# Adaptive-norm attention and mixture of experts on one core: the three-part split of q and k dealt to three engines

## The chip, the cores and the metric

The kernel runs on one core of one Trainium2 chip. The metric is device time in microseconds (us). Every time below is from one profiled execution, except where it says that it is a median of runs.

## The reference

The input x is 8 sequences of 256 tokens with 128 channels. A conditioning vector per sequence gives shifts, scales and gates (sa, ca, ga, sb, cb, gb).

```
h = layernorm(x) * (1 + ca) + sa
x = x + ga * attention(h)        # 16 heads of 8 channels, band of +-128 keys
h = layernorm(x) * (1 + cb) + sb
x = x + gb * moe(h)              # 8 experts, top 2, silu(h w1) * (h w3), then w2
```

In attention the keys before the first and after the last token are zeros that still count in the softmax's denominator: a query gets one term exp(0 - max) for each such padding key inside its band.

## The kernel before, in words

All five engines run programs of their own, in order, and meet at semaphores. Attention is a software pipeline over the 8 sequences b. Every engine loops `for step in range(-AHEAD, B + 4)` with AHEAD = 2, and inside it `for j in range(NPAIR)` with NPAIR = 8 pairs of heads. In one step the engines work on several sequences at once: sequence step + 2 is projected to q, k and v and packed, sequence step has its row maxima taken (`scores_A`, then `row_max` on VectorE), sequence step - 1 has its scores made again with the maximum taken off, its exponentials and its weighted values (`scores_B` on TensorE, `exps` on ScalarE, `mask_probs` on GpSimd, `weigh_values` on TensorE), sequence step - 2 is transposed and normalised (`o_T`, `normalise_attn`, `attn_T`), sequence step - 3 goes through the output projection, the gate and the second layernorm, and step - 4 through the router (`logits`, `top2`). "Step 4" in this text is step == 4 of this loop; it begins where VectorE takes the first row maximum of sequence 4.

q and k must be exact to nearly fp32 but are multiplied in bf16, so each is split in three bf16 parts: part 0 is the bf16 cast, part 1 the cast of the residual, part 2 the cast of what then remains. The parts lie in `parts[P, 2, 3, L]`. SyncE's queue stores them to HBM in 12 transfers (6 of part 0, 4 of part 1, 2 of part 2, line 291) and reads them back stacked along the contraction (`fill_stacks`, lines 303 and 306). Before the change ScalarE makes part 0 (`cast_part`, line 407), and VectorE does the rest: `split(b, 0)` after the row maximum of j=5 (lines 758 and 762), `split(b, 1)` after that of j=6 (line 765).

The row maxima go back into the stack of q as well: `half_max` on VectorE, `max_T` on TensorE, `m_copy` on ScalarE, and `store_max(b, half)` on SyncE's queue (line 279). TensorE's `scores_B` of j=0 waits for half 0 (semaphore `m_in0`), that of j=4 for half 1 (`m_in1`).

SyncE's queue is written out by hand, in this order in each step: `load_experts` (steps 2 to 5, 1.5 MB each, lines 311 and 312), `store_max(step-1, 1)`, `fill_stacks(step+1)`, `store_part(step+2, 0)`, `store_part(step+2, 1)`, `store_max(step, 0)`, `store_part(step+2, 2)`, `broadcast_mod_rows(step)`, the store of h2 for sequence step - 3. A wait in it holds all that stands behind it.

One bank of PSUM, `psM`, is handed from user to user (`take_psM`): the next matmul into it waits until the last reader is done. So `logits` at j=6 waits for `normalise_attn`, and `attn_T` at j=7 for the copy of the logits at the head of `top2`. After attention a routing stage and a loop over 39 tiles of tokens and experts follow, which the change doesn't touch.

## Time and profile before

| | |
|---|---|
| median of 3 runs | 379.56 us (377.26 to 380.9) |
| the profiled execution | 377.73 us |
| its span in the trace | 376.0 us |
| attention, to the end of the last step | to about 200 us |
| routing and expert loop | about 200 us to 376 us |
| busy: TensorE, VectorE, ScalarE, GpSimd | 286.6, 248.8, 172.6, 167.6 us |

The span is what the trace shows; the execution's time is 1.73 us longer. A busy time is a share of one engine's program; engines overlap. In the rows, PE is TensorE, PEld its weight loads, DVE VectorE, ACT ScalarE, POOL GpSimd and SPq the queue of SyncE. A row of a timeline gives start and duration, then in brackets how long the engine had been idle and which instruction released it.

### The profile page before, as it was taken

Reading aid. Unit: us, or ns where it says so; the run is one execution under the profiler, and the core shown is the slowest. Engines: PE = TensorE matmul, PEld = TensorE weight load, DVE = VectorE, ACT = ScalarE, POOL = GpSimd, SP = SyncE. Lnnn points to the kernel's source line nnn. Section 1 sums busy time; section 2 is a strip of 40 time slices with the busy share of each in tenths; the row PEclk is TensorE's granted clock in tenths of the full one; section 3 lists DMA queues with packets and bytes.
Section 4 is the critical chain, followed back from the end, with each engine's and each line's share of the span. In section 5 each row is a group of like instructions: output and inputs, shape, how many; then the busy total and the mean of one; then the engine's idle time right before and its main releaser. Section 6 shows DMA issues by size and latency. Waiting matters only on the chain. (4 is left out here: it accounts for less than half of the span.)

```text
span 376.0 us, 7095 instructions
## 1 busy us (share of the span) xinstructions
PE 286.6 (76%) x2281; PEld 207.8 (55%) x2281; DVE 248.8 (66%) x699; ACT 172.6 (46%) x360; POOL 167.6 (45%) x247
## 2 busy tenths in 40 slices
PE   4647798999889989999862349899888888888400
PEld 2223354455545545555441239888888888888400
DVE  5749787889986797987467964355555555444165
ACT  7312366666564746676710123444444444444150
POOL 3400143346452445556630242666566656664321
PEclk9999699999996989999975557999999999999955
DMA  4566355876676634101000001111111111111182
GB/s 113 149 159 149 79 133 163 219 216 152 189 190 181 169 97 110 58 1 51 17 15 14 1 22 23 42 44 42 35 42 42 42 37 40 42 42 28 38 241 84
DMA packets 38008, 32.98 MB, mean 88 GB/s; under 512 B 4456, under 2 KB 31992, under 8 KB 37984
## 3 DMA queue, kind: packets, MB, share of 16 engines
q1 hardware_dynamic: 35168, 27.17, 27.3%
q0 software_dynamic: 2496, 5.12, 5.2%
q10 hardware_dynamic: 320, 0.40, 0.4%
q8 instruction: 12, 0.20, 0.2%
q14 instruction: 12, 0.10, 0.1%
HBM read 21.64 MB, written 10.96 MB: 87 GB/s over the span
## 5 line engine op out<-in xcount | busy, mean ns | idle before, releaser
L788 DVE TENSOR_REDUCE negm<-psA 128x4 f32<-128x1024 f32 x64 | 78.1, 1222 | 20.7 <-PE psA L1157 19.7
L428 ACT ACTIVATE probs<-psB 128x512 f32<-128x512 f32 x128 | 72.3, 596 | 41.8 <-PE psB L1179 41.4
L576 POOL TENSOR_SCALAR_AFFINE_SELECT probs<-probs 128x512 f32<-128x512 f32 x64 | 42.3, 686 | 62.9 <-ACT probs L428 62.8
L1314 PE MATMUL psA<-kd,probs 128*128 128x128 f32 x416 | 54.5, 287 | 13.0 <-DVE kd L1019 12.6
L666 POOL DMA_INDIRECT y_d<-kd,sca_idx x39 | 40.7, 1044 | 43.9 <-ACT kd L492 37.7
L1314 PEld LDWEIGHTS psA<-kd,probs 128*128 128x128 f32 x416 | 51.3, 201 | 15.3 <-DVE kd L1019 14.7
L1154 PE MATMUL psA<-kd,qs 96*128 96x512 bf16 x128 | 49.6, 409 | 7.2 <-DMA kd<-stack_d 5.2
L1179 PE MATMUL psB<-qs,kd 98*128 98x256 bf16 x256 | 47.1, 283 | 1.9 <-DMA qs<-mT 1.1
L1019 DVE COPY kd<-psO 128x128 f32<-128x128 f32 x39 | 11.4, 292 | 55.2 <-remote 27.0
L661 POOL DMA_INDIRECT kd<-h_d,gat_idx x39 | 38.1, 976 | 18.5 <-issue 9.1
L1323 PE MATMUL psM<-probs,kd 128*128 128x128 f32 x312 | 41.3, 275 | 0.4 <-ACT kd L492 0.4
L1199 PE MATMUL psO<-probs,vx 128*32 128x256 f32 x512 | 38.0, 395 | 0.3 <-POOL probs L576 0.3
L1323 PEld LDWEIGHTS psM<-probs,kd 128*128 128x128 f32 x312 | 37.9, 192 | 0.6 <-DVE kd L1025 0.6
L496 ACT COPY probs<-w_sb 128x512 f32 x39 | 24.1, 619 | 29.1 <-issue 29.0
L1157 PE MATMUL psA<-mask_b,ident_b 128*128 128x256 bf16 x128 | 37.0, 289 | 0.0
L1179 PEld LDWEIGHTS psB<-qs,kd 98*128 98x128 bf16 x256 | 24.2, 103 | 16.5 <-ACT probs L428 3.4
L1154 PEld LDWEIGHTS psA<-kd,qs 96*128 96x128 bf16 x128 | 13.1, 102 | 30.6 <-issue 10.5
L492 ACT COPY kd<-psM 128x128 f32<-128x128 f32 x39 | 10.4, 266 | 40.9 <-PE psM L1323 34.2
L1314 PE MATMUL psB<-kd,probs 128*128 128x128 f32 x208 | 25.4, 275 | 0.0
L1314 PEld LDWEIGHTS psB<-kd,probs 128*128 128x128 f32 x208 | 24.3, 192 | 0.0
L1031 DVE COPY probs<-w_sb 128x512 f32 x39 | 16.8, 430 | 5.3 <-issue 5.2
L1199 PEld LDWEIGHTS psO<-probs,vx 128*32 128x32 f32 x512 | 12.0, 109 | 13.5 <-issue 9.9
(186 smaller groups left out, 410.1 us busy)
## 6 DMA issues: line engine op xcount, KB each, us to landing
stack_d<-parts SPq DMA_DIRECT2D x96, 64.0 KB, 2.1
w_sb<-in_L_ffn_experts_w_dram SPq DMA_DIRECT2D x12, 512.0 KB, 6.5
qs<-stack_d SPq DMA_DIRECT2D x8, 384.0 KB, 4.1
kd<-stack_d SPq DMA_DIRECT2D x16, 192.0 KB, 4.8
mod_sb<-mod_d SPq DMA_DIRECT2D x8, 320.0 KB, 4.2
probs<-y_d SPq DMA_DIRECT2D x8, 256.0 KB, 5.0
h_d<-h SPq DMA_DIRECT2D x8, 128.0 KB, 1.8
out_dram<-probs SPq DMA_DIRECT2D x4, 256.0 KB, 2.3
```

The source lines that it names most:

```text
L428: nc.scalar.activation(probs[:, kt, n % PRING], psB[:, kt, :].rearrange("p (h q) -> p h q", h=H2), ACT.Exp).then_inc(s["exped"], 1)
L496: nc.scalar.copy(w3_t[:, r], w3_sb[:, bass.ds(e, 1), :].rearrange("c o i -> c (o i)")).then_inc(s["w3_ready"], 1)
L576: nc.gpsimd.affine_select(out=u, in_=u, compare_op=ALU.is_ge, fill=0.0, base=0, pattern=[[0, 2 * H2], [-sign, P]], channel_multiplier=sign ...
L661: pool.indirect_dma_start(xs[:, r], None, h2_d, bass.IndirectOffsetOnAxis(ap=gat_idx[:, n:n + 1], axis=0)).then_inc(gathered[r], 16)
L666: pool.indirect_dma_start(y_d, bass.IndirectOffsetOnAxis(ap=sca_idx[:, n:n + 1], axis=0), ys[:, r], None).then_inc(scattered[r], 16)
L788: nc.vector.tensor_reduce(negm[:, b % 2, :, :, j], psA[:, n % 2].rearrange("p q (h k) -> p q h k", h=H2), AX.X, ALU.max, negate=True).then ...
L1154: nc.tensor.matmul(psA[:, n % 2, qt, :].rearrange("p (h k) -> p h k", h=H2), qs[0:SROWS, r, j, qt * P:(qt + 1) * P], kd[0:SROWS, r, :, j, ...
L1157: last = nc.tensor.matmul(psA[:, n % 2, qt, :].rearrange("p (h k) -> p h k", h=H2)[:, :, off:off + P], ident_b[:], mask_b[:, qt], start=Fa ...
L1179: last = nc.tensor.matmul(psB[:, kt, h * L:(h + 1) * L], kd[0:SROWS + H2, r, h, j, kt * P:(kt + 1) * P], qs[0:SROWS + H2, r, j, :], start= ...
L1199: last = nc.tensor.matmul(psO[32 * g:32 * g + 32, half, :], vx[:, b % VRING, kt, j, h, :], probs[:, kt, j, h, :], start=(piece == 0), stop ...
L1314: last = nc.tensor.matmul(ps[:, k * P:(k + 1) * P], w[:, r, k * P:(k + 1) * P], xsT[:, r], start=True, stop=True)
L1323: last = nc.tensor.matmul(psY, hid[:, r, k * P:(k + 1) * P], w2_t[:, r, k * C:(k + 1) * C], start=(k == 0), stop=(k == NC - 1))
```

## The change

- `cast_part1`: part 1's cast goes from VectorE to ScalarE, ahead of the exponentials of j=6.
- `part2`: the last subtraction goes to GpSimd, behind the masks of j=7, for sequences 2 to 7; for the first two it stays on VectorE (`part2_first`). `residual` is what is left on VectorE.
- `pad_term` goes from VectorE to GpSimd, at j=4 behind `h2_scale`.
- VectorE's paired small operations become one each, or two for four in `values`; for this the bias of v is loaded twice side by side, one transfer more at the start.

```diff
...
@@ -267,7 +267,8 @@
...
             sp.dma_start(wv_sb[:], wv).then_inc(s["wv_in"], 16)
-            sp.dma_start(bv_sb[:], bv.partition_broadcast(P)).then_inc(s["wv_in"], 16)
+            for kt in range(2):
+                sp.dma_start(bv_sb[:, kt], bv.partition_broadcast(P)).then_inc(s["wv_in"], 16)
...
@@ -281,10 +282,7 @@
...
-                if part == 0:
-                    sp.wait_ge(s["part_cast"], b + 1)
-                else:
-                    sp.wait_ge(s["residuals"], 3 * b + 1 + part)
+                sp.wait_ge(s[("part_cast", "part1_cast", "part2_ready")[part]], b + 1)
...
@@ -393,7 +391,7 @@
...
                 if b >= 1:
-                    act.wait_ge(s["residuals"], 3 * b)
+                    act.wait_ge(s["resid_ready"], b)
...
@@ -405,6 +403,10 @@
...
                 nc.scalar.copy(parts[:, :, 0, :], qkf[:]).then_inc(s["part_cast"], 1)
+            def cast_part1(b):
+                act.wait_ge(s["resid_ready"], b + 1)
+                nc.scalar.copy(parts[:, :, 1, :], resid[:]).then_inc(s["part1_cast"], 1)
...
@@ -413,7 +415,7 @@
...
                 if b >= 3:
-                    act.wait_ge(s["den_steps"], 3 * (b - 2))
+                    act.wait_ge(s["pad_ready"], b - 2)
...
@@ -464,6 +466,8 @@
...
                         cast_part(step + AHEAD)
+                    if j == (4 if step == -AHEAD else 6) and has(step + AHEAD):
+                        cast_part1(step + AHEAD)
...
@@ -575,6 +579,23 @@
...
                                             pattern=[[0, 2 * H2], [-sign, P]], channel_multiplier=sign).then_inc(s["masked"], 1)
+            def part2(b):
+                pool.wait_ge(s["part1_cast"], b + 1)
+                nc.gpsimd.tensor_tensor(parts[:, :, 2, :], resid[:], parts[:, :, 1, :], ALU.subtract).then_inc(s["part2_ready"], 1)
+            def pad_term(b):
+                pool.wait_ge(s["emin_ready"], 2 * b + 2)
+                if b == 0:
+                    pool.wait_ge(s["consts"], 5)
+                if b >= 1:
+                    pool.wait_ge(s["den_steps"], 2 * b - 1)
+                for qt in range(2):
+                    last = nc.gpsimd.tensor_scalar(
+                        den[:, 0, qt, :].rearrange("p (f q h) -> p f h q", f=2, h=H2),
+                        emin[:, b % 3, :, qt], npad[:, qt:qt + 1], 0.0, ALU.mult, ALU.add)
+                last.then_inc(s["pad_ready"], 1)
...
@@ -640,6 +661,10 @@
...
                         h2_shift(step - 3)
+                    if j == 4 and has(step - 2):
+                        pad_term(step - 2)
+                    if j == 7 and step > 1 - AHEAD and has(step + AHEAD):
+                        part2(step + AHEAD)
...
@@ -751,33 +776,30 @@
...
-            def split(b, i):
-                if i == 0:
-                    dve.wait_ge(s["part_cast"], b + 1)
-                    nc.vector.tensor_tensor(resid[:], qkf[:], parts[:, :, 0, :], ALU.subtract).then_inc(s["residuals"], 1)
-                    dve.wait_ge(s["residuals"], 3 * b + 1)
-                    if b >= 1:
-                        dve.wait_ge(s["parts_stored"], NSTORES * 16 * b)
-                    nc.vector.tensor_copy(parts[:, :, 1, :], resid[:]).then_inc(s["residuals"], 1)
-                else:
-                    dve.wait_ge(s["residuals"], 3 * b + 2)
-                    nc.vector.tensor_tensor(parts[:, :, 2, :], resid[:], parts[:, :, 1, :], ALU.subtract).then_inc(s["residuals"], 1)
+            def residual(b):
+                dve.wait_ge(s["part_cast"], b + 1)
+                if b >= 1:
+                    dve.wait_ge(s["part2_ready"], b)
+                nc.vector.tensor_tensor(resid[:], qkf[:], parts[:, :, 0, :], ALU.subtract).then_inc(s["resid_ready"], 1)
+            def part2_first(b):
+                dve.wait_ge(s["part1_cast"], b + 1)
+                nc.vector.tensor_tensor(parts[:, :, 2, :], resid[:], parts[:, :, 1, :], ALU.subtract).then_inc(s["part2_ready"], 1)
...
             def values(b):
...
-                    dve.wait_ge(s["wv_in"], 32)
+                    dve.wait_ge(s["wv_in"], 48)
...
-                for kt in range(2):
-                    for par in range(H2):
-                        last = nc.vector.tensor_tensor(
-                            vx[:, b % VRING, kt, :, par, D * par:D * par + D],
-                            psM[:, kt * C:(kt + 1) * C].rearrange("p (q h d) -> p q h d", h=H2, d=D)[:, :, par, :],
-                            bv_sb[:].rearrange("p (q h d) -> p q h d", h=H2, d=D)[:, :, par, :], ALU.add)
+                for par in range(H2):
+                    last = nc.vector.tensor_tensor(
+                        vx[:, b % VRING].rearrange("p k q h c -> p (k q) h c")[:, :, par, D * par:D * par + D],
+                        psM[:, 0:2 * C].rearrange("p (q h d) -> p q h d", h=H2, d=D)[:, :, par, :],
+                        bv_sb[:].rearrange("p k (q h d) -> p (k q) h d", h=H2, d=D)[:, :, par, :], ALU.add)
...
             def row_max(b, j):
@@ -795,53 +817,33 @@
...
-                for qt in range(2):
-                    last = nc.vector.tensor_scalar(negmb[:, b % 2, half, qt], negm[:, b % 2, qt, :, 4 * half:4 * half + 4],
-                                                   0.0, None, ALU.min)
-                last.then_inc(s["half_max"], 1)
-            def pad_term(b):
-                dve.wait_ge(s["emin_ready"], 2 * b + 2)
-                if b == 0:
-                    dve.wait_ge(s["consts"], 5)
-                for qt in range(2):
-                    last = nc.vector.tensor_scalar(
-                        den[:, 0, qt, :].rearrange("p (f q h) -> p f h q", f=2, h=H2),
-                        emin[:, b % 3, :, qt], npad[:, qt:qt + 1], None, ALU.mult)
-                last.then_inc(s["den_steps"], 1)
+                nc.vector.tensor_scalar(negmb[:, b % 2, half], negm[:, b % 2, :, :, 4 * half:4 * half + 4],
+                                        0.0, None, ALU.min).then_inc(s["half_max"], 1)
...
             def normalise_attn(b):
-                dve.wait_ge(s["den_steps"], 3 * b + 1)
+                dve.wait_ge(s["pad_ready"], b + 1)
...
-                for qt in range(2):
-                    ps = late(b)[:, qt * 256:(qt + 1) * 256].rearrange("p (q r) -> p q r", r=VCOL)
-                    last = nc.vector.tensor_tensor(
-                        den[:, 1, qt, :].rearrange("p (q h) -> p q h", h=H2), ps[:, :, 16:18],
-                        den[:, 0, qt, :].rearrange("p (q h) -> p q h", h=H2), ALU.add)
-                last.then_inc(s["den_steps"], 1)
-                dve.wait_ge(s["den_steps"], 3 * b + 2)
+                ps = late(b)[:, 0:2 * L].rearrange("p (q r) -> p q r", r=VCOL)
+                nc.vector.tensor_tensor(den[:, 1].rearrange("p t (q h) -> p (t q) h", h=H2), ps[:, :, 16:18],
+                                        den[:, 0].rearrange("p t (q h) -> p (t q) h", h=H2), ALU.add).then_inc(s["den_steps"], 1)
+                dve.wait_ge(s["den_steps"], 2 * b + 1)
...
-                dve.wait_ge(s["den_steps"], 3 * b + 3)
+                dve.wait_ge(s["den_steps"], 2 * b + 2)
...
-                for qt in range(2):
-                    ps = late(b)[:, qt * 256:(qt + 1) * 256].rearrange("p (q r) -> p q r", r=VCOL)[:, :, 0:16]
-                    last = nc.vector.tensor_tensor(
-                        attn[:, qt, :].rearrange("p (q h d) -> p q h d", h=H2, d=D),
-                        ps.rearrange("p q (h d) -> p q h d", d=D),
-                        den[:, 2, qt, :].rearrange("p (q h o) -> p q h o", h=H2, o=1).broadcast_to([P, NPAIR, H2, D]),
-                        ALU.mult)
-                last.then_inc(s["normed"], 1)
+                nc.vector.tensor_tensor(
+                    attn[:].rearrange("p t (q h d) -> p (t q) h d", h=H2, d=D),
+                    ps[:, :, 0:16].rearrange("p q (h d) -> p q h d", d=D),
+                    den[:, 2].rearrange("p t (q h o) -> p (t q) h o", h=H2, o=1).broadcast_to([P, 2 * NPAIR, H2, D]),
+                    ALU.mult).then_inc(s["normed"], 1)
...
             def gate_attn(b):
...
-                for t in range(2):
-                    nc.vector.tensor_tensor(t1[:, t], late(b)[:, t * C:(t + 1) * C], mod_sb[:, b, 0, :],
-                                            ALU.mult).then_inc(s["t1_ready"], 1)
+                nc.vector.tensor_tensor(t1[:], late(b)[:, 0:2 * C].rearrange("p (t c) -> p t c", c=C),
+                                        mod_sb[:, b, 0:1, :].broadcast_to([P, 2, C]), ALU.mult).then_inc(s["t1_ready"], 2)
...
             def x1_last(b):
...
@@ -923,8 +925,8 @@
...
                     if j == 4 and step == -AHEAD:
-                        split(0, 0)
-                        split(0, 1)
+                        residual(0)
+                        part2_first(0)
...
@@ -941,12 +943,10 @@
...
                         h2_last(step - 3)
-                    if j == 4 and has(step - 2):
-                        pad_term(step - 2)
                     if j == 5 and step > -AHEAD and has(step + AHEAD):
-                        split(step + AHEAD, 0)
-                    if j == 6 and step > -AHEAD and has(step + AHEAD):
-                        split(step + AHEAD, 1)
+                        residual(step + AHEAD)
+                    if j == 7 and step == 1 - AHEAD:
+                        part2_first(1)
...
```

## Rows read from the trace of the kernel before

**Rows 1.** Windows, one step each (steps 2 to 6): span, busy times, clock, DMA, GB/s.
```profile
58.62:77.36 18.74, 17.25 (x148) 9.07 (x148) 15.14 (x35) 12.48 (x26) 6.10 (x11) 1.00 0.71 190
77.36:96.88 19.52, 17.71 (x154) 10.00 (x154) 17.48 (x43) 12.46 (x27) 10.89 (x18) 1.00 0.65 178
96.88:120.11 23.23, 20.97 (x160) 11.74 (x161) 18.77 (x56) 12.68 (x27) 10.32 (x18) 0.87 0.73 187
120.11:142.15 22.04, 20.13 (x160) 11.26 (x159) 17.56 (x49) 12.67 (x27) 9.57 (x16) 0.90 0.56 157
142.15:158.57 16.42, 16.28 (x150) 9.09 (x149) 14.82 (x42) 10.69 (x23) 8.35 (x17) 1.00 0.32 81
```

**Rows 2.** Timeline of TensorE, step 4, j=6 and j=7: start, us, engine line [idle before].
```profile
112.60 0.61 PE L1236 MATMUL psM<-gate_sb,h2T 128*128 128x8 f32 x4 [1.37 <-DVE attn L830]
...
114.42 0.69 PE L1215 MATMUL psM<-ident,attn 128*128 128x128 f32 x2 [0.40 <-DVE lg L886]
114.90 0.63 PE L1154 MATMUL psA<-kd,qs 96*128 96x512 bf16 x1
```

**Rows 3.** Timeline of VectorE, step 4, j=5 to j=7.
```profile
110.03 0.67 DVE L758 TENSOR_TENSOR resid<-qkf,parts 128x512 f32<-128x512 f32 x1
110.73 0.74 DVE L762 CAST parts<-resid 128x512 bf16<-128x512 f32 x1
...
113.60 0.68 DVE L765 TENSOR_TENSOR parts<-resid,parts 128x512 bf16<-128x512 f32 x1
```

**Rows 4.** Timeline of TensorE, steps 1 to 4: first scores of a step or half.
```profile
41.64 1.04 PE L1179 MATMUL psB<-qs,kd 98*128 98x256 bf16 x4 [0.28 <-DMA qs<-mT]
...
58.75 0.44 PE L1126 MATMUL psM<-ident,xn 128*128 128x128 f32 x2 [1.00 <-DVE xn L706]
...
68.72 0.39 PE L1179 MATMUL psB<-qs,kd 98*128 98x256 bf16 x2 [0.78 <-DMA qs<-mT]
...
106.47 0.38 PE L1179 MATMUL psB<-qs,kd 98*128 98x256 bf16 x2
```

**Rows 5.** Timeline of SyncE's queue, from steps 1 to 4.
```profile
58.16 1.51 SPq L291 DMA_DIRECT2D stack_d<-parts  x2
...
60.34 0.94 SPq L311 DMA_DIRECT2D w_sb<-in_L_ffn_experts_w_dram  x2
...
95.60 1.17 SPq L291 DMA_DIRECT2D stack_d<-parts  x2
...
97.92 1.03 SPq L311 DMA_DIRECT2D w_sb<-in_L_ffn_experts_w_dram  x2
```

**Rows 6.** Page, DMA issues: count, KB each, us to landing.
```profile
w_sb<-in_L_ffn_experts_w_dram SPq DMA_DIRECT2D x12, 512.0 KB, 6.5
```

**Rows 7.** Timeline of GpSimd, steps 1 and 3, the masks after j=7.
```profile
57.40 1.22 POOL L576 TENSOR_SCALAR_AFFINE_SELECT probs<-probs 128x512 f32<-128x512 f32 x2 [1.49 <-ACT probs L428]
...
95.66 1.22 POOL L576 TENSOR_SCALAR_AFFINE_SELECT probs<-probs 128x512 f32<-128x512 f32 x2 [1.49 <-ACT probs L428]
```

**Rows 8.** Groups by form, GpSimd's additions.
```profile
L589 POOL TENSOR_TENSOR x_sb<-t,x_sb 128x256 f32<-128x256 f32 x7 | 5.1, 732 | 11.6 <-DVE t L843 11.6
...
L583 POOL TENSOR_TENSOR x_sb<-x_sb,mod_sb 128x128 f32<-128x128 f32 x16 | 7.0, 454 | 0.0
```

**Rows 9.** Groups by form, VectorE and ScalarE.
```profile
L777 DVE TENSOR_TENSOR vx<-psM,bv_sb 128x64 f32<-128x64 f32 x32 | 4.9, 217 | 2.7 <-PE psM L1142 2.5
...
L407 ACT CAST parts<-qkf 128x512 bf16<-128x512 f32 x8 | 4.9, 619 | 1.4 <-DMA stack_d<-parts 1.3
...
L762 DVE CAST parts<-resid 128x512 bf16<-128x512 f32 x8 | 4.7, 584 | 0.3
```

**Rows 10.** Timeline of all engines, step 9.
```profile
191.40 0.65 DVE L809 TENSOR_SCALAR den<-emin,npad 128x16 f32<-128x16 f32 x2
191.57 0.87 POOL L601 TENSOR_TENSOR h2m<-xn,mod_sb 128x128 f32<-128x128 f32 x2 [0.72 <-DVE xn L881]
...
193.31 0.69 PE L1215 MATMUL psA<-ident,attn 128*128 128x128 f32 x2 [2.13 <-DVE attn L830]
```

More of the change, by code:

```diff
@@ L127, in adaln_attention_moe @@
         bqk = sb("bqk", [P, 4])
-        bv_sb = sb("bv_sb", [P, C])
+        bv_sb = sb("bv_sb", [P, 2, C])
         stats = sb("stats", [P, NT, 6])
@@ L240, in adaln_attention_moe @@
             "ln1_steps veps_ok rstd_ok stack_const0 stack_const1 vx_zero vx_ones "
-            "xn_ready xnT_ps hT_ready qk_ps qkf_ready part_cast residuals parts_stored v_ps v_ready "
+            "xn_ready xnT_ps hT_ready qk_ps qkf_ready part_cast part1_cast resid_ready part2_ready parts_stored v_ps v_ready "
             "scoresA rowmax half_max mT_ps mT_ready emin_ready m_in0 m_in1 "
-            "scoresB exped masked pv o_ready oT_ps den_steps normed aT_ps aT_ready op_ps t1_ready xg_ready x1_ready "
+            "scoresB exped masked pv o_ready oT_ps pad_ready den_steps normed aT_ps aT_ready op_ps t1_ready xg_ready x1_ready "
             "ln2_steps rs2_ready xn2_ready h2m_ready h2_ready h2T_ps h2T_ready lg_ps lg_ready top_ready h2_stored0 h2_stored1"
@@ L1138, in project_v @@
                 if b == 0:
-                    pe.wait_ge(s["wv_in"], 32)
+                    pe.wait_ge(s["wv_in"], 48)
                 take_psM("v_ready", b + 1)
```

## The prediction

> **What bounds the kernel now.** I read the windows first, one for each step of attention, since only attention is changed. In step 6, with nothing left to project or pack, TensorE is busy for 16.28 of 16.42 us: it sets that step, and step 7 is like it. Steps 2 to 5 last 18.74 to 23.23 us, and TensorE's idle time in them is 1.49, 1.81, 2.26 and 1.91 us. In steps 4 and 5 the granted clock is 0.87 and 0.90 as well: part of the time was at the lower of its two levels, 1.2 GHz [rows 1]. Reckoned at full speed that loses 0.13 x 23.23 = 3.0 and 0.10 x 22.04 = 2.2 us. So there are 7.5 us of idle time and 5.2 us of clock in these four steps, and nothing else that a better division of work could win; VectorE's 75 to 90% matters only where TensorE waits for it.
>
> Then I read TensorE's timeline at the end of step 4 for who releases it. It is idle for 1.37 us until attn is normalised, then for 0.40 us until the logits are copied, and from 114.90 the same matmuls take 0.63 us each [rows 2]: the clock fell behind these two waits. VectorE shows why: residual and cast, 0.67 + 0.74 us, stand ahead of the normalisation, and the third part, 0.68 us, ahead of the copy [rows 3]. Elsewhere a wait of 1.00 us stands alone, and the matmul behind it is at full speed with 0.44 us [rows 4].
>
> Last I read the waits that do not end on a compute engine. Scores of j=4 in step 2 waited 0.78 us for a transfer, the second half of the row maxima; in step 4 they start at 106.47 without a wait. The first scores of step 1 also waited for such a store, the other half, 0.28 us [rows 4].
>
> **The change, part by part.** *VectorE.* Per step it loses the cast (0.58 us mean; 0.74 us in step 4), the third part (0.68 us) [rows 3, 9] and the padding term (0.65 us in step 9) [rows 10]. Of the merges, four adds of values (217 ns each alone, overlapping in a row) become two: 0.1 us; row maxima, denominators, attn and gate give some 0.3 us together, my estimate from the same overlap. In all 2.1 to 2.4 us a step. On TensorE's path lie only the cast (0.74) and about 0.1 us ahead of the normalisation, and the subtraction ahead of the copy: the wait of 1.37 becomes 0.4 to 0.6 and that of 0.40 becomes 0.2 us. If the two waits no longer throw the clock, 3.0 + 2.2 us come back too.
>
> *ScalarE.* One cast more, 0.62 us as its twin [rows 9]. It stands in front of the exponentials of j=6 and waits for the residual, and behind it TensorE waits for the exponentials' PSUM. ScalarE has some 12.7 busy us in 23 [rows 1]; while the residual is made it has nothing to do. Cost 0 to 0.2 us a step, taken as 0.1 within the waits below. Part 1's four stores go out behind part 0's six in either case.
>
> *The extra load of the bias and the first steps.* One issue of some 0.5 us on SyncE's queue at the start, where the queue later waits for the first cast anyway: nothing. Step 0 gets about 1.3 us off VectorE, but the first scores of step 1 wait for the stored row maxima already [rows 4], and that store stands behind the same stores of parts: gain nothing; step 1 likewise, up to 0.3 us.
>
> *GpSimd, the third part.* The trace has no such subtraction of 512 columns on GpSimd. Bounds: 0.68 us, VectorE's own [rows 3], and 1.46 us, twice the 732 ns of 256 columns. The two additions (454 ns for 128 columns, 732 for 256) give 176 ns + 2.17 ns a column, so 1.29 us [rows 8]; I take 1.3. The Trainium skill, GPSIMD Engine Reference, section "3.1 Elementwise — side-by-side cycle accounting", gives such an operation 1.96 times VectorE's time, which would be an estimate of 1.33 us here; the sum would not move.
>
> Its length is not the point, its place is. It comes behind the masks of j=7, which wait for the last exponentials: they start at 95.66 and end at 96.88 [rows 7]. So the third part is ready at about 98.2. Its stores went out at 95.60, and they head a row on SyncE's queue: stores of part 2, broadcast of the modulation, the store of h2, the expert weights at 97.92 [rows 5], and behind these the second half of the row maxima. All that moves by 98.2 - 95.6 = 2.6 us. In step 2 it moves by 57.40 + 1.22 + 1.3 + 0.05 - 58.16 = 1.8 us [rows 5, 7].
>
> The row maxima are a small store behind 1.5 MB of weights. In step 2 TensorE could go on 68.72 - 60.34 = 8.4 us after the first of the weights was issued [rows 4, 5]; the weights take 6.5 us to land [rows 6], and the third of them is issued some 1.0 us after the first, so the delay is at least 7.5 us. The Trainium skill says in DMA: Bandwidth & Descriptors, section "Queues, rings and completion order", that each DMA engine consumes descriptors in ring order; by that rule a small store cannot pass the weights, and the row of 68.72 agrees. Without it the store would land early and the stall below would be zero.
>
> With 8.4 us, step 4's weights go out at 100.5, the maxima are there at 108.9, and TensorE wants them at 106.47 less some 0.4 us from shorter waits before: a stall of 2.8 us. With 7.5 us and the shorter subtraction it is 1.3 us. Step 2: 0.78 + 1.8 = 2.6 us. Step 3 has one issue less ahead of the weights: 2.4. Step 5: as step 4, 2.8. While TensorE stands, VectorE catches up, so the later waits shrink further. Step by step, idle plus clock loss now against then, with 0.4, 0.5, 1.2 and 0.7 us for waits that remain: step 2, 1.5 to 3.0; step 3, 1.8 to 2.9; step 4, 5.3 to 4.0; step 5, 4.1 to 3.5. Sum +1.5 +1.1 -1.3 -0.6 = +0.7 us.
>
> *GpSimd, the padding term.* In steps 1 to 7 it fits between `h2_scale` and the next masks. In step 9 it does not: `h2_scale` runs until 191.57 + 0.87 = 192.44, two small operations follow (no row for them; at most the 0.65 us of VectorE, at least 0.2; I take 0.4), and only then may VectorE normalise, which it now does behind its own padding term, from 192.05. TensorE is already waiting for it there, 2.13 us [rows 10]. Cost 0.8 us, less 0.2 of merges: +0.6 (0.2 to 0.9). Sum so far +1.3 us.
>
> *The clock.* A stall of 2.4 to 2.8 us in one piece is longer than the 1.37 + 0.40 us that preceded a fall [rows 2], and longer than the 1.00 us that did not [rows 4]. So I expect it to fall behind these stalls in about two of the four steps. One fall cost 3.0 or 2.2 us; less some 0.6 us of waits that it covers, 2.0 each: +4 us. Together +5.3: 377.73 + 5.3 = 383.0 against the profiled execution, and with the 1.83 us by which the median lies above it, 384.9; I say 384.5.
>
> **The rivals.** *B, the stall comes and the clock holds.* +1.3 us: 380.9. For it: I know no place where one wait of this length stands alone in full work.
>
> *C, faster.* The same relief with a short stall. It decides at about 1.2 us: between the 1.00 us behind which the clock held and the 1.77 us behind which it fell. With 1.0 us in each step (the maxima landing 7.5 us after the weights, or the third part ready near 0.7 us) idle and clock are 1.4, 1.5, 2.2 and 1.7 us, against 1.5, 1.8, 5.3 and 4.1: -5.9, +0.6 at the end, so -5.3: 374.3. For it: steps 3 and 4 of before show no wait for the maxima, so the delay might be under 8.4 us there. Against it: the bounds must all fall on one side.
>
> *D, the clock falls in all four steps, or the last step costs more.* +9: 388.5.
>
> **How the numbers follow.** Forecast A (two or so falls) 0.40, D 0.07, B 0.25, C 0.28. A measurement of this kernel tells about 1% from no change, 3.8 us. A lies over that by its middle (part of it under), D over, B within, C partly within. Faster 0.25, same 0.31, slower 0.44. The range takes in C and nearly D, 373.5 to 389.5; the forecast's own is 382 to 388.
>
> **What would show it.** In the profile after: TensorE's wait for the store of the row maxima at j=4 in steps 2 to 5 grows from 0.8 us in all to about 10; the cast on ScalarE 0.62 us, the subtraction on GpSimd 1.3 us; the waits for attn and logits in steps 4 and 5 nearly gone; the low-clock stretch behind j=4 instead of j=6; in step 9 VectorE waits some 0.8 us for GpSimd. I am wrong if the maxima land less than 7.5 us after the weights are issued, or if GpSimd's masks of j=7 end before the store of part 2 was due.

## The result and the profile after

The changed kernel takes 386.57 us, the median of 4 runs (384.71 to 390.52), where the kernel before took 378.55 us in 4 runs on the same chip (377.26 to 380.9). The ratio is 1.0205, with a 95% interval of 1.0164 to 1.0247: 2% slower. One of the 4 runs, the one of 390.52 us, was in a slower state of the chip and is left out of the ratio. The profiled run of the changed kernel is one of 385.87 us with a span of 384.1 us, against 376.0 us before; the two profiles differ by 8.1 us.

These are the windows of the changed kernel for steps 2 to 5, in the columns of [rows 1]: span, busy time of TensorE, its weight loads, VectorE, ScalarE and GpSimd, granted clock, DMA share, GB/s.

```profile
59.92:81.63 21.71, 18.67 (x148) 9.94 (x148) 14.06 (x24) 13.23 (x27) 8.04 (x16) 0.92 0.62 165
81.63:102.52 20.89, 17.82 (x154) 9.92 (x154) 15.71 (x32) 13.21 (x28) 11.13 (x22) 1.00 0.62 168
102.52:126.26 23.74, 19.91 (x158) 10.86 (x158) 17.19 (x46) 13.20 (x28) 11.71 (x23) 0.93 0.57 153
126.26:147.44 21.18, 18.32 (x160) 10.59 (x161) 15.39 (x39) 13.31 (x28) 9.89 (x20) 1.00 0.66 172
```

Against [rows 1], VectorE has 1.1 to 2.2 us less to do in each step, and still three of the four steps are longer (step 5 is 0.9 us shorter). TensorE's idle time, span less busy, is 3.04, 3.07, 3.83 and 2.86 us where it was 1.49, 1.81, 2.26 and 1.91. The clock now falls in steps 2 and 4 instead of 4 and 5. The list of waits names what TensorE waits for; its columns are the us of all such waits, their number and the longest, from 40 to 200 us:

```profile
PE psB L1179 <- DMA qs<-mT: 11.9, 6, 2.8
...
DVE den L827 <- POOL den L595: 5.1, 4, 2.9
```

The first row is the row maxima, coming back from memory. Two of the six waits are for their first half, at j=0 of steps 1 and 2 (1.79 us, which was 0.28, and 0.84 us, which was none). The other four are for the second half: the first scores of j=4 in steps 2 to 5. In TensorE's timeline they answer to the third of [rows 4], which had 0.78 us, and to the fourth, which had no wait:

```profile
71.72 0.39 PE L1179 MATMUL psB<-qs,kd 98*128 98x256 bf16 x2 [1.72 <-DMA qs<-mT]
...
93.89 0.39 PE L1179 MATMUL psB<-qs,kd 98*128 98x256 bf16 x2 [2.44 <-DMA qs<-mT]
...
115.08 0.39 PE L1179 MATMUL psB<-qs,kd 98*128 98x256 bf16 x2 [2.80 <-DMA qs<-mT]
...
138.35 0.39 PE L1179 MATMUL psB<-qs,kd 98*128 98x256 bf16 x2 [2.34 <-DMA qs<-mT]
```

Their sum is 9.30 us. Why the store comes late is to be read on SyncE's queue in step 4, which answers to [rows 5], and on GpSimd, which answers to [rows 7]:

```profile
104.26 1.18 SPq L289 DMA_DIRECT2D stack_d<-parts  x2
105.48 0.59 SPq L320 DMA_DIRECT2D mod_sb<-mod_d  x1
106.11 0.43 SPq L343 DMA_DIRECT2D h_d<-h  x1
106.59 1.03 SPq L309 DMA_DIRECT2D w_sb<-in_L_ffn_experts_w_dram  x2
107.66 0.47 SPq L310 DMA_DIRECT2D w_sb<-in_L_ffn_experts_w_dram  x1
108.17 0.68 SPq L280 DMA_DIRECT2D qs<-mT  x1
```

```profile
101.89 1.22 POOL L580 TENSOR_SCALAR_AFFINE_SELECT probs<-probs 128x512 f32<-128x512 f32 x2 [1.62 <-ACT probs L430]
103.08 1.15 POOL L585 TENSOR_TENSOR parts<-resid,parts 128x512 bf16<-128x512 f32 x1
```

The masks of j=7 end at 103.1, the third part follows until 104.23, and the stores of part 2 leave 0.03 us later. Everything below stands behind them in the program of SyncE: modulation, h2, the three issues of expert weights, and at 108.17 the row maxima. TensorE goes on at 115.08, 8.49 us after the first of the weights. In steps 2, 3 and 5 this delay is 8.20, 8.04 and 8.61 us.

The trace also has the moment at which each store's semaphore is raised. In steps 2 to 5 the store of the row maxima lands 5.05, 6.49, 6.86 and 7.01 us after its own issue, and TensorE starts 0.04 to 0.05 us behind it. The kernel before was already at the edge: in steps 3 and 4 the maxima landed 8.29 and 8.39 us after the first of the weights, in step 4 at 106.31, and TensorE wanted them at 106.47.

The groups by form price the moved operations, in the columns of [rows 9]:

```profile
L585 POOL TENSOR_TENSOR parts<-resid,parts 128x512 bf16<-128x512 f32 x6 | 6.9, 1154 | 5.9 <-ACT parts L409 5.9
...
L409 ACT CAST parts<-resid 128x512 bf16<-128x512 f32 x8 | 4.9, 616 | 8.0 <-DVE resid L783 7.9
...
L595 POOL TENSOR_SCALAR den<-emin,npad 128x16 f32<-128x16 f32 x16 | 4.2, 280 | 0.0
```

The subtraction of 512 columns takes 1.15 us on GpSimd, the cast on ScalarE 0.62 us, and a padding operation of 16 columns 0.28 us on GpSimd.

Two smaller losses lie outside these steps. The first is at the start, where the bias is loaded twice. SyncE's timeline and VectorE's:

```profile
9.27 2.55 SPq L275 DMA_DIRECT2D gate_sb<-in_L_ffn_gate_dram  x1
11.86 7.65 SPq L289 DMA_DIRECT2D stack_d<-parts  x12
```

```profile
12.86 0.49 DVE L715 BATCH_NORM_STATS2 stats<-x_sb 128x6 f32<-128x128 f32 x2 [3.61 <-DMA x_sb<-in_L_attn_x_dram]
```

The issue of the small gate load takes 2.55 us (0.92 before), the stores of the first part leave at 11.86 (10.95 before), and x of the next batch comes so late that VectorE waits 3.61 us for it. The first row maximum is taken at 27.94 instead of 26.86 us. The second is in the tail, step 9, and answers to [rows 10]:

```profile
197.06 0.86 POOL L622 TENSOR_TENSOR h2m<-xn,mod_sb 128x128 f32<-128x128 f32 x2 [0.72 <-DVE xn L883]
197.90 0.53 POOL L595 TENSOR_SCALAR den<-emin,npad 128x16 f32<-128x16 f32 x2
...
198.46 0.19 DVE L827 TENSOR_TENSOR den<-psA,den 128x32 f32<-128x32 f32 x1 [1.48 <-POOL den L595]
...
199.55 0.69 PE L1215 MATMUL psA<-ident,attn 128*128 128x128 f32 x2 [2.86 <-DVE attn L834]
```

GpSimd does the padding term only after `h2m`, VectorE waits 1.48 us for it, and TensorE waits 2.86 us for attn where it waited 2.13. From the last row maximum to the first matmul of the routing it is 33.05 us against 31.94.

By stretches, the 8.1 us are: start 1.1, steps 0 and 1 0.2, steps 2 to 5 4.0, steps 6 and 7 -0.2, tail 1.1, and 1.9 in routing and expert loop, whose code is the same in both kernels.

### The profile page after: what moved, and what is told of

Same layout as the page of the kernel before. It is cut to its first block and busy times, and to the rows that moved or that the text cites. A ratio compares the mean times of both kernels' runs of the same rounds, so it can differ in the third digit from the quotient of the medians.

```text
span 384.1 us, 7052 instructions
## 1 busy us (share of the span) xinstructions
PE 286.1 (74%) x2281; PEld 207.9 (54%) x2281; DVE 234.8 (61%) x613; ACT 177.8 (46%) x368; POOL 176.2 (46%) x269
## 3 DMA queue, kind: packets, MB, share of 16 engines
HBM read 21.71 MB, written 10.96 MB: 85 GB/s over the span
## 5 line engine op out<-in xcount | busy, mean ns | idle before, releaser
L580 POOL TENSOR_SCALAR_AFFINE_SELECT probs<-probs 128x512 f32<-128x512 f32 x64 | 39.4, 639 | 59.6 <-ACT probs L430 59.4
L1025 DVE TENSOR_TENSOR kd<-psA,kd 128x512 f32<-128x512 f32 x26 | 17.8, 686 | 2.3 <-PE psA L1314 1.6
```

Of the source, the lines that this page charges most:

```text
L580: nc.gpsimd.affine_select(out=u, in_=u, compare_op=ALU.is_ge, fill=0.0, base=0, pattern=[[0, 2 * H2], [-sign, P]], channel_multiplier=sign ...
```

## The experiments

Each kernel was timed against runs of the kernel before on the same chip. The chips differ (medians of the kernel before: 378.06 us for the first four experiments, 375.17 for the next four, 375.21 for the last two), so ratios are to be compared and not times. "First row maximum" below is the start of step 0's first one, and the sum of steps 2 to 5 runs from the first row maximum of step 2 to that of step 6: 83.53 us before and 87.52 changed. It comes from one profiled execution of each kernel.

**The third part back on VectorE.** Of the change all else stays.

```diff
+                    if j == 6 and step > -AHEAD and has(step + AHEAD):
+                        part2_first(step + AHEAD)      # VectorE
...
-                    if j == 7 and step > 1 - AHEAD and has(step + AHEAD):
-                        part2(step + AHEAD)            # GpSimd
```

> The changed kernel with the third part back on VectorE, ahead of j=7's work; all else as changed. Theory Q (the third part's stores, late on SyncE's queue, push the expert weights and behind them the row maxima): TensorE's wait for the row maxima at j=4 of steps 2 to 5 falls from 9.3 us to 1 to 2 us, and the time to 1.000 to 1.008 of the kernel before; what is left over 1.000 is the start (+1.1 us) and the last steps (+1.1 us). Rival G (the added cast on ScalarE and the padding term on GpSimd cost it, wherever the third part is): it stays at 1.015 to 1.022.

Measured: 375.46 us, ratio 0.9948 (0.9911 to 0.9984). One wait for the row maxima at j=4 is left, in step 2, as long as before:

```profile
70.76 0.39 PE L1173 MATMUL psB<-qs,kd 98*128 98x256 bf16 x2 [0.81 <-DMA qs<-mT]
```

Steps 2 to 5 take 77.07 us. So the one moved subtraction turns the rest of the change from 0.5% faster into 2% slower. The wait is a little under the expected 1 to 2 us. The ratio is 0.5% under the expected range, which allowed 1.1 us for the start; in this kernel the start cost 0.2 us (first row maximum at 27.02).

**The expert weights behind the row maxima.** The changed kernel, with the two weight loads of a step issued after the loads of the stacks instead of ahead of the row maxima. GpSimd keeps the third part.

```diff
-                if 2 <= step < 2 + E // 2:
-                    load_experts(2 * (step - 2))
...
                     fill_stacks(step + AHEAD - 1)
+                if 2 <= step < 2 + E // 2:
+                    load_experts(2 * (step - 2))
```

> The changed kernel, third part on GpSimd as changed, but the expert weights issued behind the row maxima and the filling of the stacks of the same step. Theory Q: the third part is as late as before, yet the row maxima have no weights in front of them; the wait at j=4 falls to under 0.5 us in all, the clock holds behind j=4, and the time is 0.995 to 1.006 of the kernel before. Rival L (what costs is that the third part itself is late, because the stacks are filled late): no gain, 1.015 to 1.022. Rival G: the same, 1.015 to 1.022.

Measured: 372.17 us, ratio 0.9861 (0.9827 to 0.9896). SyncE's timeline in step 4, then the windows of steps 2 to 5:

```profile
97.74 1.18 SPq L289 DMA_DIRECT2D stack_d<-parts  x2
98.96 0.59 SPq L320 DMA_DIRECT2D mod_sb<-mod_d  x1
99.59 0.43 SPq L343 DMA_DIRECT2D h_d<-h  x1
100.29 0.68 SPq L280 DMA_DIRECT2D qs<-mT  x1
101.07 0.33 SPq L301 DMA_DIRECT2D qs<-stack_d  x1
101.44 0.89 SPq L304 DMA_DIRECT2D kd<-stack_d  x2
102.38 0.94 SPq L309 DMA_DIRECT2D w_sb<-in_L_ffn_experts_w_dram  x2
```

```profile
59.35:77.71 18.36, 17.09 (x148) 9.15 (x148) 14.06 (x24) 13.06 (x27) 8.06 (x16) 1.00 0.70 195
77.71:96.00 18.29, 17.64 (x154) 10.00 (x154) 15.63 (x33) 13.08 (x28) 11.56 (x22) 1.00 0.69 191
96.00:115.82 19.82, 18.27 (x158) 10.36 (x158) 17.25 (x46) 13.41 (x28) 12.13 (x22) 1.00 0.66 185
115.82:134.84 19.02, 18.34 (x160) 10.66 (x161) 15.29 (x39) 13.19 (x28) 10.27 (x19) 1.00 0.69 191
```

The stores of part 2 leave as late as in the changed kernel, behind the masks, 1.74 us after the start of step 4 in both; the row maxima now go out at 100.29, ahead of the weights at 102.38. No wait at j=4 is left in any step, and the clock is 1.00 in all four. They take 75.49 us, 12.0 less than in the changed kernel. The store of the maxima now lands 2.0 to 2.5 us after its issue, and not 5.0 to 7.0. So the late third part does its harm through the weights in front of the maxima. The gain is larger than was expected (0.995 to 1.006).

**The kernel before with the same move of the weights.** It separates what the order alone brings from what the relief of VectorE brings once the order is mended.

```diff
-                if 2 <= step < 2 + E // 2:
-                    load_experts(2 * (step - 2))       # ahead of the row maxima
...
+                if 2 <= step < 2 + E // 2:
+                    load_experts(2 * (step - 2))       # behind fill_stacks
```

> The kernel before with the expert weights issued behind the row maxima and the stacks. Theory Q: only the wait of 0.78 us in step 2 is there to be won; 0.996 to 1.001. If the weights in this place hold up the stores of the parts instead, 1.003 to 1.010.

Measured: 377.06 us, ratio 0.9967 (0.9946 to 0.9987). Windows of steps 4 and 5:

```profile
97.55:118.83 21.28, 18.37 (x158) 10.38 (x158) 19.02 (x57) 12.56 (x27) 10.29 (x17) 1.00 0.64 181
118.83:139.32 20.49, 18.23 (x159) 10.50 (x160) 17.52 (x49) 12.56 (x27) 8.85 (x15) 1.00 0.61 175
```

The waits for attn and for the logits are still there in both steps, 1.37 and 0.40 us, as in [rows 2]. But the clock did not fall behind them in this execution; over the ten runs the mean granted clock goes from 0.896 to 0.921, and this one is at the upper end. Steps 2 to 5 take 79.25 us here (to the first row maximum of step 6 at 139.49; the window shown ends 0.17 us earlier) and 75.49 us with the relief of VectorE: in these two profiles the relief is worth 3.8 us, and the two ratios differ by 1.1%. The changed kernel hides it behind its stalls. The ratio is in the expected range. Of the 4.3 us between 79.25 and the 83.53 of the kernel before, most is the clock that did not fall, and the medians show only 0.3%.

**The kernel before with only the third part on GpSimd.** Cast, padding term and all small operations stay as before.

```diff
-                    if j == 6 and step > -AHEAD and has(step + AHEAD):
-                        split(step + AHEAD, 1)         # VectorE
...
+                    if j == 7 and step > 1 - AHEAD and has(step + AHEAD):
+                        part2(step + AHEAD)            # GpSimd, behind the masks
```

> The kernel before with one part of the change alone: the third part of sequences 2 to 7 on GpSimd behind the masks of j=7. Theory Q: the waits for the row maxima at j=4 are 8 to 11 us in all, as in the changed kernel, and the time is 1.008 to 1.020 of the kernel before. Rival G: VectorE is relieved of 0.68 us a step, so 0.990 to 1.003.

Measured: 388.69 us, ratio 1.0278 (1.0248 to 1.0307). The same four first scores of j=4:

```profile
70.03 0.61 PE L1187 MATMUL psB<-qs,kd 98*128 98x256 bf16 x2 [2.15 <-DMA qs<-mT]
...
93.67 0.61 PE L1187 MATMUL psB<-qs,kd 98*128 98x256 bf16 x2 [2.65 <-DMA qs<-mT]
...
117.31 0.61 PE L1187 MATMUL psB<-qs,kd 98*128 98x256 bf16 x2 [2.60 <-DMA qs<-mT]
...
141.43 0.61 PE L1187 MATMUL psB<-qs,kd 98*128 98x256 bf16 x2 [3.11 <-DMA qs<-mT]
```

The loss comes with this one move and is larger without the relief: 10.51 us of waits, and behind each of the four the two scores take 0.61 us instead of 0.39, which is the lower clock. Steps 2 to 5 take 95.29 us. The waits are in the expected range of 8 to 11 us; the time lies over it (1.008 to 1.020), as the clock fell in all four steps.

**The third part ahead of the masks of j=7.** The changed kernel; the subtraction stays on GpSimd and is only issued before the masks.

```diff
+                    if j == 7 and step > 1 - AHEAD and has(step + AHEAD):
+                        part2(step + AHEAD)
                     if j % 2 == 1 and has(step - 1):
                         mask_probs(step - 1, j - 1)
...
-                    if j == 7 and step > 1 - AHEAD and has(step + AHEAD):
-                        part2(step + AHEAD)
```

> The changed kernel with GpSimd's third part issued ahead of the masks of j=7 instead of behind them, so that it no longer waits for the last exponentials; same instruction, same engine, weights where they were. Theory Q: its place and not its length costs; the waits for the row maxima at j=4 fall from 9.3 us to 0.5 to 2 us, 0.985 to 1.000 of the kernel before. Rival: the subtraction of 1.15 us on GpSimd itself costs (port, masks pushed later): over 1.005.

Measured: 372.38 us, ratio 0.9921 (0.9898 to 0.9944). SyncE in step 4:

```profile
96.39 1.17 SPq L289 DMA_DIRECT2D stack_d<-parts  x2
...
98.71 1.01 SPq L309 DMA_DIRECT2D w_sb<-in_L_ffn_experts_w_dram  x2
```

The stores leave 0.44 us ahead of the start of step 4 (96.83), and not 1.74 us behind it; only step 2 keeps a wait at j=4, of 0.55 us, and steps 2 to 5 take 77.03 us. All is as expected. The subtraction still takes 1.15 us: its place did the harm, not its length.

**The padding term back on VectorE**, with the weights behind the row maxima. The function moves as a whole; this is its one operation.

```diff
-                    last = nc.gpsimd.tensor_scalar(
+                    last = nc.vector.tensor_scalar(
                         den[:, 0, qt, :].rearrange("p (f q h) -> p f h q", f=2, h=H2),
-                        emin[:, b % 3, :, qt], npad[:, qt:qt + 1], 0.0, ALU.mult, ALU.add)
+                        emin[:, b % 3, :, qt], npad[:, qt:qt + 1], None, ALU.mult)
```

> The kernel of e2 with the padding term back on VectorE. Tail theory: VectorE's waits for GpSimd's padding term in steps 6 to 9 (5.1 us in the changed kernel's trace) go; of them only step 9's lies on the end's path, so the time from the last row maximum to the routing's first matmul falls by 0.6 to 1.3 us, and the median is 0.8 to 1.3 us under e2's 372.2. Rival: VectorE is loaded again by 0.65 us a step, and that gives as much back in steps 2 to 5: 372 to 374.

Measured: 369.94 us, ratio 0.9858 (0.9821 to 0.9895); the time is that of the late weights alone. In the trace the tail gives 1.5 us back: last row maximum to routing is 31.01 us, against 32.53 with the late weights alone. The wait for attn in step 9, from the chain of waits, is:

```profile
PE psA L1213 <- DVE attn L830: 2.0, 1, 2.0
```

It was 2.86 us in the changed kernel. In return, two waits of about 0.5 us for attn are back in the steps, which take 75.95 us. The expected 0.8 to 1.3 us are not seen in the time: a gain of this size can't be told from none here.

**The bias loaded once**, with the weights behind the row maxima; the additions of the values are four again.

```diff
-            for kt in range(2):
-                sp.dma_start(bv_sb[:, kt], bv.partition_broadcast(P)).then_inc(s["wv_in"], 16)
+            sp.dma_start(bv_sb[:], bv.partition_broadcast(P)).then_inc(s["wv_in"], 16)
```

> The kernel of e2 with the bias of v loaded once and four additions in place of two. Theory: the second load of 64 KB costs about 1 us at the start (x arrives 2 us later and the stores of the parts begin 0.9 us later in the changed kernel); the first row maximum comes at 26.8 to 27.0 us instead of 27.6, and the median is 0.6 to 1.1 us under e2's 372.2. Rival: the starts differ by chance, and four additions cost 0.1 us a step: 372 to 373.

Measured: 369.30 us, ratio 0.9840 (0.9807 to 0.9872), the best point value of all. SyncE at the start:

```profile
7.97 0.85 SPq L274 DMA_DIRECT2D gate_sb<-in_L_ffn_gate_dram  x1
11.05 7.66 SPq L288 DMA_DIRECT2D stack_d<-parts  x12
```

The gate load is issued in 0.85 us and the parts' stores leave at 11.05. In all five kernels with one load the gate issue takes 0.66 to 0.92 us and the first row maximum is at 26.76 to 26.95 us; in the seven with two loads it is 1.77 to 2.95 us and 26.82 to 27.94. The extra load costs 0 to 1.1 us, 0.6 on the mean, and steps 2 to 5 don't miss the merge (75.47 us). The ratio is 0.2% under that of the late weights alone, in the expected direction, but the intervals overlap: the gain is read from the traces and not from the time.

**All four together:** late weights, the third part ahead of the masks, the padding term on VectorE, one bias load. Of its edit, the order of the two queues:

```diff
                     fill_stacks(step + AHEAD - 1)
+                if 2 <= step < 2 + E // 2:
+                    load_experts(2 * (step - 2))
...
+                        part2(step + AHEAD)
                     if j % 2 == 1 and has(step - 1):
```

> The weights behind the stacks, the third part on GpSimd ahead of the masks, the padding term on VectorE, one bias load. If the gains add: 0.980 to 0.984 of the kernel before (370.3 to 372). If the weights' new place has already taken all that the third part's place can give, it is at e2's ratio less the tail's and the start's 1 to 2 us, 0.981 to 0.985; not distinguishable by time, but the store of part 2 in the trace is then 2.5 us earlier.

Measured: 369.96 us, ratio 0.985 (0.9818 to 0.9883). It is no better than the late weights with one of the others: the gains don't add. Once the row maxima no longer stand behind the weights, the place of the third part brings nothing, and may cost a little: the stores of part 2 leave 1.7 us earlier in step 4 (2.5 were expected), and still steps 2 to 5 take 77.01 us, 1.1 more than in the kernel with the padding term on VectorE and the third part behind the masks.

**The cast of part 1 back on VectorE**, with the weights behind the row maxima.

```diff
-                nc.scalar.copy(parts[:, :, 1, :], resid[:]).then_inc(s["part1_cast"], 1)
+                nc.vector.tensor_copy(parts[:, :, 1, :], resid[:]).then_inc(s["part1_cast"], 1)
```

> The kernel of e2 (0.986) with part 1's cast back on VectorE, behind the residual and ahead of the normalisation; the third part stays on GpSimd. Theory R (the change's gain is the relief of VectorE ahead of the normalisation): TensorE waits again for attn before the logits in steps 4 and 5, 1.0 to 1.4 us each, the clock may fall behind it, and steps 4 and 5 are 1 to 3 us longer each than e2's 19.82 and 19.02; 0.990 to 1.000. Rival: the cast on ScalarE, in front of the exponentials, costs as much as it relieves: 0.984 to 0.988.

Measured: 369.80 us, ratio 0.9859 (0.981 to 0.9909). VectorE's and TensorE's timelines in step 4:

```profile
108.22 0.70 DVE L778 TENSOR_TENSOR resid<-qkf,parts 128x512 f32<-128x512 f32 x1
108.96 0.43 DVE L782 CAST parts<-resid 128x512 bf16<-128x512 f32 x1
```

```profile
110.39 0.61 PE L1235 MATMUL psM<-gate_sb,h2T 128*128 128x8 f32 x4 [0.39 <-DVE attn L833]
```

With the padding term gone from VectorE the cast takes 0.43 us there, not the 0.74 of [rows 3], and TensorE waits 0.39 us for attn and not 1.37. The 0.65 us of the padding term and the 0.31 us of the cast together come near the 0.98 us that the wait has lost; that it lost them by just these two is not shown. The steps take 75.86 us against 75.49, and the ratio is the rival's: moving the cast to ScalarE brings nothing that can be measured once the padding term is off VectorE. It does no harm either.

**The third part back on VectorE, with the late weights.**

```diff
+                    if j == 6 and step > -AHEAD and has(step + AHEAD):
+                        part2_first(step + AHEAD)      # VectorE
...
-                        part2(step + AHEAD)            # GpSimd
```

> The kernel of e2 with the third part back on VectorE (0.68 us at j=6, ahead of the copy of the logits). Theory R: the wait for that copy returns with 0.2 to 0.5 us in steps 4 and 5 and for the normalised x with 0.3 us in the others, 1 to 1.5 us in all: 0.987 to 0.992. Rival: the third part on GpSimd gave nothing once the weights are out of the way: 0.984 to 0.987.

Measured: 371.24 us, ratio 0.9875 (0.9824 to 0.9925). Two waits of 0.57 us for the logits are back; the steps take 76.03 us. So in the traces a third part on GpSimd is 0.5 us better than one on VectorE, when no weights queue behind it. The time doesn't decide between the two expectations: the interval covers both.

## Why the prediction was right

The forecast was 384.5 us, slower; measured was 386.57. In ratios it is 1.013 against 379.56 us and 1.0205 measured. The stated range of 373.5 to 389.5 us took in nearly every outcome, faster ones too, so to lie in it says little; 386.57 also lies in the forecast's own 382 to 388. The mechanism is the one forecast, and the sizes are to be read term by term.

*The place of the third part, and the queue behind it.* Right. The expert weights of step 4 go out 8.67 us later than in [rows 5], of which the start of the step explains 5.64 (102.52 against 96.88); the rest, 3.0, is the delay forecast as 2.6. Undoing either end of the chain (subtraction ahead of the masks, or weights behind the row maxima) takes the stalls away, all but 0.55 us, and the one move alone on the kernel before makes them.

*The delay behind the weights.* Forecast 8.4 us with 7.5 as the lower bound; measured 8.04 to 8.61. The landings of the kernel before say the same, 8.29 and 8.39 us in steps 3 and 4, so these steps were no sign of a shorter delay, as rival C took them. The trace agrees with the ring order that the Trainium skill gives in DMA: Bandwidth & Descriptors, section "Queues, rings and completion order": with the weights moved behind it the same store lands in 2.0 to 2.5 us and makes TensorE wait in no step. But "cannot pass the weights" is too strong: in the changed kernel the store landed 0.05 to 2.6 us ahead of the last of the three loads in front of it.

*The stalls.* Forecast 2.6, 2.4, 2.8 and 2.8; measured 1.72, 2.44, 2.80 and 2.34, in all 9.30 against 10.6. Step 2 was off by most, as TensorE itself came to j=4 later there: 10.08 us after the start of the step, and 9.32 in the kernel before.

*The clock.* Forecast: falls in about two of four steps. It fell in two, 2 and 4. At full speed the losses are 0.08 x 21.71 = 1.7 and 0.07 x 23.74 = 1.7 us. The choice of which steps was not forecast, and could not be from the length of a stall: the clock fell behind one of 1.72 us and not behind one of 2.44. That it fell twice is one execution; the profiled one has the highest mean clock of the four runs, 0.910, and the others 0.879 to 0.903.

*Steps 2 to 5 in sum.* Forecast +0.7 and +4 for the clock, so +4.7; measured +4.0. The parts agree too: idle time 13.4 us forecast and 12.8 measured, new clock loss 4.0 and 3.4, and the 5.2 us of clock loss of before given back as forecast.

*The subtraction, the cast, VectorE's relief.* The subtraction was forecast at 1.3 us and measured at 1.15, which is 1.67 times VectorE's 0.69. The estimate of 1.33 us, from the 1.96 times that the Trainium skill gives in GPSIMD Engine Reference, section "3.1 Elementwise — side-by-side cycle accounting", for a longer addition in fp32, was too high here; the sum did not use it. The cast on ScalarE was 0.62 us as forecast. For the relief of VectorE 2.1 to 2.4 us a step were forecast and 1.65 on the mean measured (14.06, 15.71, 17.19 and 15.39 against [rows 1]). The 0.74 us for the cast on VectorE, which the prediction took as the price of a cast, was that of a cast that starts while GpSimd's masks run; started first it takes 0.43 (last section). That the wait of 1.37 us needed the cast's removal was wrong: with cast and padding term both on VectorE it is 1.37, with either of them (and the merges) gone 0.4 to 0.5, in kernels without the stalls.

*The terms mis-sized.* "One issue of some 0.5 us ... nothing" for the extra bias load: it cost 1.1 us in this profile (0 to 1.1 over the runs). It was the issue that I priced; the load itself, and what it holds up behind it, were left out. Steps 0 and 1 then gained nothing, as forecast: the wait for the first half of the maxima in step 1 grew from 0.28 to 1.79 us. "+0.6" for the padding term in the tail: measured +1.1. The two small operations, taken as 0.4, are 0.53 us, and `h2m` ahead of them starts 18.49 us after the last row maximum and not 18.09. VectorE's share of 75 to 90%, in the first paragraph, is 80 to 90% by [rows 1]; nothing rests on it.

*What no term held.* 1.9 us in the routing and the expert loop. Over all runs this stretch, the same code in each kernel, varies from 168.6 to 172.9 us (170.6 before, 172.5 after). It doesn't go with the change: the kernel before with the weights moved took 172.0 us and the one with only the third part moved 172.5, while the six kernels with the change or most of it that were timed on the two other chips took 168.6 to 170.2. The difference between the two profiles grows evenly through the loop. So it is taken as chance; its cause stays open. The two profiles differ by 8.1 us and the terms summed to 5.3: of the 2.8 us between them this stretch is 1.9, start and first steps 1.3, tail 0.5, and steps 2 to 7 are 0.9 the other way. That the forecast falls short by no more than 2.1 us in the median is thus partly luck: misses of both signs, and a stretch that nobody forecast.

*The rivals.* The faster one (C) needed a short stall; it is what the experiments made by taking the queue out of the way: 0.986. Its sign and size, -5.3 us, came near what the relief gives without the stall (5.9 us less than the kernel before, 372.17 against 378.06), though not term by term: C put idle time and clock of steps 2 to 5 at 5.9 us less, and they became 8.0 us shorter. B, the stall with a steady clock, happened in steps 3 and 5 only. D, falls in all four steps, is what the kernel before does with the third part on GpSimd alone; that this took 388.69 us, near D's 388.5, is no test of D, which is about the changed kernel.

## What to carry to other kernels

When a step moves to another engine, ask first what it will stand behind there and what stands behind its result, on each queue down to the last consumer: here 1.15 us of subtraction, started late, cost 9.3 us of waits, because it held back 1.5 MB of weights and the 4 KB store that stood behind them. Put large loads that nobody needs yet behind the small transfers of the step: the store landed in 2.0 to 2.5 us ahead of the weights and in 5.0 to 7.0 behind them. That reordering and the change together take 1.4% off, where the change alone adds 2.0% and the reordering alone takes 0.3%. When three edits relieve one engine, ask what the last of them still brings: cast, padding term and third part, each put back alone on VectorE, cost 0.4 to 0.5 us in the steps. What one of them alone would bring was not run.

## What the runs showed of the hardware

The granted clock did not follow the length of one wait. In the changed kernel it fell to 1.2 GHz in steps 2 and 4, at 72.4 and 116.8, which is 0.7 and 1.7 us after waits of 1.72 and 2.80 us had ended, and it held behind 2.44 and 2.34 us. In the kernel with only the third part moved it fell in all four steps, at 69.5, 93.4, 117.3 and 141.2, and so within the waits of 2.15, 2.65, 2.60 and 3.11 us or at their end. In the kernel before it fell at 114.1 and 138.0, around the wait of 0.40 us that follows the one of 1.37; in that kernel with the weights moved the same two waits left it at 2.4 GHz. What else decides, no run here settles.

One more partition-broadcast load of 64 KB ahead in the queue made the issue of the next small load last 1.8 to 2.95 us on SyncE instead of 0.7 to 0.9. An issue's own time is thus no bound on what a transfer costs the queue.

The cast of 128x512 elements on VectorE has two durations. In the kernel before it is 0.74 or 0.75 us in the four steps in which a mask on GpSimd had begun up to 0.8 us earlier, and 0.43 us in the other four. In one of these the masks began 0.02 us after the cast; there the cast kept its 0.43 us, and the two masks took 1.49 us instead of 1.22. With the cast back on VectorE and the padding term on GpSimd ahead of the masks, three of the four slow casts took 0.43 us, each begun 0.06 us ahead of the masks, and the masks 1.44. GpSimd's timeline of that kernel in step 4, beside the cast at 108.96 shown above:

```profile
108.10 0.97 POOL L590 TENSOR_SCALAR den<-emin,npad 128x16 f32<-128x16 f32 x2
109.02 1.44 POOL L575 TENSOR_SCALAR_AFFINE_SELECT probs<-probs 128x512 f32<-128x512 f32 x2
```

So a cast that begins ahead of a mask runs at full speed, and the mask waits. To begin first is not always enough: in the kernel before, in the step of [rows 3], the masks begin 0.08 us ahead of the residual, and yet the residual keeps its 0.67 us and the two masks take 2.02:

```profile
109.95 2.02 POOL L576 TENSOR_SCALAR_AFFINE_SELECT probs<-probs 128x512 f32<-128x512 f32 x2 [0.59 <-ACT probs L428]
```

The first mask alone takes 1.24 us of these, near the 0.67 of the residual and its own 0.6 in a row; the cast behind the residual begins while that mask still runs. The Trainium skill, Trainium Architecture — The Big Picture, section "What this means for kernel authors", says that only VectorE and GpSimd contend for a shared pair of ports and that it is "an exclusive lock (not a bandwidth split)"; the rows agree, as the two take turns and the residual is no slower than alone.
